# Expert weights split once and kept on chip, and unrolled expert tiles of 128 rows

## The reference

```python
x = x + attn(layernorm(x), W_write, W_read, decay, log_alpha)   # recurrent over chunks
x = x + ffn(layernorm(x), gate_w, w1, b1, w2, b2)

# ffn: 4096 rows, D = 256, F = 1024, E = 8, TOP_K = 2
probs = softmax(x @ gate_w.T); topk_probs, topk_idx = top_k(probs, 2)
h = gelu(w1[topk_idx] @ x + b1[topk_idx])      # per chosen expert
y = w2[topk_idx] @ h + b2[topk_idx]
out = sum over the 2 of y * topk_probs
```

## Time and profile before

| | |
|---|---|
| median of 3 runs | 681.88 us (680.44 to 682.3) |
| span of the profiled execution | 644.7 us, mean granted TensorE clock 0.961 |
| own time of the profiled execution | not listed; the median is 37.2 us over its span |
| PE / PEld busy | 585.2 us (91%) / 502.0 us (78%) |
| DVE busy | 560.0 us (87%) |
| ACT busy | 414.1 us (64%) |
| POOL busy | 291.4 us (45%) |
| recurrent part and tables | up to 222.4 us |
| expert part, PE's matmuls | 222.4 to 632.8 us |

### The profile page before, as it was taken

One profiled execution on the slowest core, in us unless ns is written; L12 is line 12 of the kernel. 1 busy time (PEld: TensorE's weight loads), 2 busy tenths in 40 slices (PEclk: granted clock), 3 DMA queues, 4 the chain that ended last, 5 costly groups with the idle time before them and its releaser, 6 DMA issues.

```text
span 644.7 us, 17218 instructions
## 1 busy us (share of the span) xinstructions
PE 585.2 (91%) x5368; PEld 502.0 (78%) x5368; DVE 560.0 (87%) x1323; ACT 414.1 (64%) x819; POOL 291.4 (45%) x301
## 2 busy tenths in 40 slices
PE   3899889888894499999999999999999999999992
PEld 2677677676673288888888888888888888888882
DVE  4699898998886799999999998999999999999971
ACT  6454554543541487878777777777787877777751
POOL 4145777677667414443343434243433334342433
PEclk9899997999896599999999999999999999999997
DMA  6567464466122415253434434252524343443422
GB/s 231 185 201 280 134 229 165 161 224 205 60 94 96 97 29 84 48 76 51 73 57 67 71 53 77 47 82 47 77 49 74 51 73 57 67 72 52 80 29 33
DMA packets 87098, 63.46 MB, mean 98 GB/s; under 512 B 56224, under 2 KB 79392, under 8 KB 87072
## 3 DMA queue, kind: packets, MB, share of 16 engines
q1 hardware_dynamic: 72768, 44.23, 25.4%
q0 software_dynamic: 14304, 18.92, 17.0%
HBM read 27.36 MB, written 25.53 MB: 82 GB/s over the span
## 4 chain that ended last, share of the span: by engine, by line
PE 61%; POOL 12%; issue 11%; DVE 8%; DMA 5%; ACT 2%; POOLq 0%; DVEq 0%; ACTq 0%; SPq 0%
PE psum L1213 28%; PE psum L1194 28%; POOL sent_rows L469 6%; DMA out<-arena 3%; POOL tiny L448 2%; DMA sent_rows<-arena,tiny 2%; DVE arena L903 2%; POOL arena L477 2%; POOL out L494 1%; PE psum L1139 1%; POOL tiny L445 1%; PE psum L1113 1%; PE psum L1142 1%; DVE arena L819 1%; PE psum L1103 1%
## 5 line engine op out<-in xcount | busy, mean ns | idle before, releaser
L1194 PE MATMUL psum<-arena 128*128 128x256 f16 x1872 | 229.7, 273 | 0.7 <-ACT arena L631 0.7
L1213 PE MATMUL psum<-arena 128*128 128x256 f16 x1872 | 229.5, 273 | 0.4 <-DVE arena L996 0.4
L1009 DVE SCALAR_TENSOR_TENSOR arena<-weights,arena 128x1024 f16<-128x1024 f16 x156 | 190.2, 1221 | 25.0 <-issue 14.1
L494 POOL DMA_INDIRECT out<-arena x78 | 133.3, 1709 | 155.9 <-ACT arena L670 135.4
L1194 PEld LDWEIGHTS psum<-arena 128*128 128x128 f16 x1872 | 183.0, 98 | 23.1 <-DVE arena L1009 0.9
L1213 PEld LDWEIGHTS psum<-arena 128*128 128x128 f16 x1872 | 183.1, 98 | 21.9 <-DVE arena L996 0.7
L651 ACT ACTIVATE arena<-weights 128x1024 f16 x156 | 164.2, 1055 | 35.8 <-PE psum L1213 20.8
L631 ACT ACTIVATE arena<-psum,arena 128x256 f32<-128x256 f32 x312 | 130.7, 470 | 68.3 <-PE psum L1194 63.6
L996 DVE TENSOR_TENSOR arena<-arena 128x512 f16<-128x512 f32 x156 | 108.1, 693 | 5.3
L469 POOL DMA_INDIRECT sent_rows<-arena,tiny x64 | 63.7, 995 | 41.4 <-DVE tiny L778 21.6
L503 POOL COPY arena<-arena 128x2 int32<-128x2 int32 x39 | 24.4, 625 | 107.6 <-DMA out<-arena 98.8
(11 more groups left out here) (129 smaller groups left out, 566.6 us busy)
## 6 DMA issues: line engine op xcount, KB each, us to landing
weights<-in_experts SPq DMA_DIRECT2D x16, 1024.0 KB
arena<-in_b SPq DMA_DIRECT2D x39, 128.0 KB, 2.9
out<-arena SPq DMA_DIRECT2D x17, 256.0 KB, 2.4
arena<-in_x SPq DMA_DIRECT2D x16, 256.0 KB, 2.8
sent_rows<-pad SPq DMA_DIRECT2D x8, 265.0 KB, 7.5
out<-arena POOLq DMA_INDIRECT x78, 4.1
sent_rows<-arena,tiny POOLq DMA_INDIRECT x64
arena<-sent_rows SPq DMA_TRANSPOSE x39, 3.9
```

What stands on the lines that cost most here:

```text
L494: pool.indirect_dma_start(out=out, out_offset=bass.IndirectOffsetOnAxis(ap=tok_cur[:, 1 - par, c:c + 1], axis=0), in_=yout[:, 1 - par, c], ...
L1009: v.scalar_tensor_tensor(out=wcur[:, 1 - par, w + PIECE:w + 2 * PIECE], in0=weights[:, bass.ds(e * EW + part * PIECE, PIECE)], scalar=WSCA ...
L1194: last = pe.matmul(ps_h[:, s, mm], w1_of(par, k, lo, m), tileT[:, par, part], start=(n == 0), stop=(n == 3 * KD - 1))
L1213: last = pe.matmul(ps_y[:, par, c], lhs, w2_of(par, m, lo), start=(m == 0 and n == 0), stop=(m == MF - 1 and n == 2))
```

## The change

All expert weights are split in the recurrent part, two pieces a step, by ACT and DVE. The halves take the place of the f32 weights: piece j arrives one piece further on in `weights` and its halves are written behind it. So `wcur` and the splits per tile are gone. Tiles have 128 rows (NT = (8192 + 8 x 127) // 128 = 71), all loops of the expert part are written out, and PE reads the weights' halves in place, with slices that begin at a register, the expert's number. The hidden rows are handled in 2 groups of 4 blocks. `b2` of all experts is loaded once. DVE multiplies bias and result by the gate, so L670 is gone, and POOL takes the row numbers from `tile_in`, which has 8 buffers, so L503 is gone. There is one indirect addition a tile, and each waits for the one before. Tables are computed in memory that the recurrent part has freed.

The core of the diff; of removed lines only some are shown, and lines with @@ tell the place:

```diff
-TILE = 256
+TILE = 128
...
-EW = 4 * PIECE
+EW = 4 * 2 * PIECE
...
-        weights = sb("weights", [P, E * EW])
+        weights = sb("weights", [P, (NPIECE + 1) * PIECE])
+        halves = weights[:].bitcast(F16)
...
@@ SyncE, recurrent step @@
+                    reached(sp, "wlo_done", 2 * n - 3)
                     src = experts[2 * n:2 * n + 2] if is_int(n) else experts[bass.ds(2 * n, 2)]
-                    o = 2 * n * PIECE
+                    o = (2 * n + 1) * PIECE
...
@@ SyncE, expert part @@
+            sp.wait_ge(buffers_free, 1)
+            sp.dma_start(b2_all, b2.rearrange("e d -> (e d)").rearrange("(a w) -> a w", a=1).to_broadcast([P, E * D])
+                         ).then_inc(b2_in, 16)
             sp.wait_ge(pad_out, 16 * E)
+            def load_tile(i):
+                came(sp, "h_ps", i - 4, 2)
+                r = sp.value_load(tile_row_i[0:1, i:i + 1], min_val=0, max_val=E * CAP - TILE)
+                sp.dma_start_transpose(tileT[:, i % 4], sent16[bass.ds(r, TILE), 0:2 * D]).then_inc(tileT_ld[i % 4], 16)
+                if i >= 8:
+                    sp.wait_ge(added, 16 * (i - 7))
+                sp.dma_start(tile_in[:, i % 8], sent[bass.ds(r, TILE), D:ROW]).then_inc(tile_ld[i % 8], 16)
...
@@ GpSimd, expert part @@
+            def add(i):
+                came(pool, "yout_done", i)
+                pool.wait_ge(tile_ld[i % 8], (i // 8 + 1) * 16)
+                if i > 0:
+                    pool.wait_ge(added, i * 16)
+                pool.indirect_dma_start(
+                    out=out, out_offset=bass.IndirectOffsetOnAxis(ap=tile_in[:, i % 8, E:E + 1].bitcast(I32), axis=0),
+                    in_=yout[:, i % 4], in_offset=None, compute_op=ALU.add).then_inc(added, 16)
...
@@ ScalarE: called twice in each recurrent step from step 1 to 16, after the xT copies and after vals @@
+            def split_high(j, m, mp):
+                loaded(a, w_in[mp], m, mp)
+                reached(a, "wlo_done", j - 1)
+                if not is_int(j):
+                    a.sem_inc(carrier_act, 1)
+                to, frm = j * (2 * PIECE), (j + 1) * PIECE
+                to = halves[:, to:to + PIECE] if is_int(to) else halves[:, bass.ds(to, PIECE)]
+                frm = weights[:, frm:frm + PIECE] if is_int(frm) else weights[:, bass.ds(frm, PIECE)]
+                a.activation(to, frm, ACT.Copy, scale=WSCALE).then_inc(S["whi_done"], 1)
...
@@ ScalarE, expert part @@
+            def gelu(i, q):
+                came(a, "h_ps", i, 2, q)
+                came(a, "prep_done", i)
+                came(a, "split_done", i - 1, 2, q)
+                for m in range(4):
+                    last = a.activation(act[:, q, m * TILE:(m + 1) * TILE], ps_h[:, q, m], ACT.Gelu_apprx_tanh,
+                                        scale=1.0 / WSCALE, bias=b1_cur[:, i % 2, 4 * q + m:4 * q + m + 1])
...
@@ VectorE: called twice in each recurrent step, after the state's sum and after choose() @@
+            def split_low(j):
+                reached(v, "whi_done", j)
...
+                v.scalar_tensor_tensor(out=lo, in0=frm, scalar=WSCALE, in1=hi, op0=ALU.mult,
+                                       op1=ALU.subtract).then_inc(S["wlo_done"], 1)
...
@@ VectorE, expert part @@
+            def prepare(i):
+                e = v.value_load(tile_exp_i[0:1, i:i + 1], min_val=0, max_val=E - 1)
+                came(v, "act_done", i - 2, 2)
+                v.tensor_copy(b1_cur[:, i % 2], b1T[:].rearrange("p e m -> p (e m)")[:, bass.ds(e * MF, MF)])
+                v.wait_ge(tile_ld[i % 8], (i // 8 + 1) * 16)
+                came(v, "yout_done", i - 2)
...
+                v.tensor_scalar(b2_cur[:, i % 2], b2_all[:, bass.ds(e * D, D)], gate_cur[:, i % 2, 0:1], None,
+                                ALU.mult).then_inc(S2["gated_done"], 1)
+            def finish(i):
+                came(v, "l2_done", i, 2)
+                came(v, "gated_done", i)
+                if i >= 4:
+                    v.wait_ge(added, 16 * (i - 3))
+                v.scalar_tensor_tensor(out=yout[:, i % 4], in0=ps_y[:, i % 2], scalar=gate_cur[:, i % 2, 1:2],
+                                       in1=b2_cur[:, i % 2], op0=ALU.mult, op1=ALU.add).then_inc(S2["yout_done"], 1)
+            prepare(0)
+            for i in range(NT + 1):
                 if has(i):
                     split(i, 0)
+                if has(i - 1):
+                    finish(i - 1)
                 if has(i + 1):
+                    prepare(i + 1)
                 if has(i):
                     split(i, 1)
...
@@ TensorE, expert part @@
+            def w1_of(e, k, lo, m):
+                return halves[:, bass.ds(e * EW + ((2 * k + lo) * PIECE + m * P), P)]
+            def w2_of(e, m, lo):
+                return halves[:, bass.ds(e * EW + ((2 * (2 + m // 4) + lo) * PIECE + m % 4 * D), D)]
+            def first(i, e, q):
+                if q == 0:
+                    pe.wait_ge(tileT_ld[i % 4], (i // 4 + 1) * 16)
+                came(pe, "act_done", i - 1, 2, q)
+                for mm in range(4):
...
                         for lo, part in ((0, k), (0, KD + k), (1, k)):
+                            last = pe.matmul(ps_h[:, q, mm], w1_of(e, k, lo, 4 * q + mm), tileT[:, i % 4, part],
                                              start=(n == 0), stop=(n == 3 * KD - 1))
...
+            def second(i, e, q):
+                s = 2 * (i % 2) + q
+                came(pe, "split_done", i, 2, q)
+                if q == 0:
+                    came(pe, "yout_done", i - 2)
+                for mm in range(4):
+                    for n, (half, lo) in enumerate(((h_hi, 0), (h_hi, 1), (h_lo, 0))):
+                        last = pe.matmul(ps_y[:, i % 2], half[:, s, mm], w2_of(e, 4 * q + mm, lo),
...
+            for i in range(NT + 1):
                 if has(i):
+                    e_of[i] = pe.value_load(tile_exp_i[0:1, i:i + 1], min_val=0, max_val=E - 1)
+                    first(i, e_of[i], 0)
                 if has(i - 1):
+                    second(i - 1, e_of[i - 1], 0)
                 if has(i):
+                    first(i, e_of[i], 1)
                 if has(i - 1):
+                    second(i - 1, e_of[i - 1], 1)
```

More of the change, by code:

```diff
@@ L81, in constants @@
     put("token", (q % 2) * T + (q // 2) * P + p)
[L82 to L83 removed]
+    put("padtoken", TOK + p)
+    put("place", p)
     put("step", np.arange(TOK // TILE)[None, :] * TILE)
@@ L242, in build @@
         x_in = [sem(f"x_in{s}") for s in range(2)]
-        w_in = sem("w_in")
+        w_in = [sem(f"w_in{s}") for s in range(2)]
         row_out = [sem(f"row_out{s}") for s in range(2)]
@@ L321, in both @@
             return v[n * P:(n + 1) * P] if is_int(n) else v[bass.ds(n * P, P)]
[L323 to L333 removed]
         def has(i):
[L336 removed]
+            return 0 <= i < NT
         def came(eng, name, i, per=1, k=None):
[L340 removed]
+            if i >= 0:
                 eng.wait_ge(S2[name], i * per + (per if k is None else k + 1))
@@ L682, in _ @@
+            for i in range(NT):
+                gelu(i, 0)
+                gelu(i, 1)
         @block.vector
@@ L1017, in step2 @@
                     split(i, 0)
+                if has(i - 1):
+                    finish(i - 1)
                 if has(i + 1):
-                    split_low(1)
+                    prepare(i + 1)
                 if has(i):
                     split(i, 1)
-                if has(i - 1):
-                    for c in range(2):
-                        came(v, "l2_done", i - 1, 4)
-                        v.wait_ge(b2_in[1 - par], (i - 1 - (1 - par)) * 8 + 16)
-                        if not is_int(i) or i >= 3:
-                            v.wait_ge(added, (i - 2) * 32)
-                        v.scalar_tensor_tensor(out=yout[:, 1 - par, c], in0=ps_y[:, 1 - par, c], scalar=1.0 / WSCALE,
-                                               in1=b2_cur[:, 1 - par], op0=ALU.mult,
-                                               op1=ALU.add).then_inc(S2["ybias_done"], 1)
@@ L1048, in step2 @@
-                if has(i):
-                    split(i, 3)
-            stage_two(v, step2)
         @block.tensor
@@ L1175, in _ @@
                 pe.matmul(psum[:, 0, :], ident16[:], proj16[:, 0, 0], start=True, stop=True)
[L1176 to L1190 removed]
+            pe.wait_ge(S["wlo_done"], NPIECE)
+            def w1_of(e, k, lo, m):
[7 more added lines that the diff above has]
+                for mm in range(4):
                     n = 0
@@ L1193, in first @@
                         for lo, part in ((0, k), (0, KD + k), (1, k)):
-                            last = pe.matmul(ps_h[:, s, mm], w1_of(par, k, lo, m), tileT[:, par, part],
+                            last = pe.matmul(ps_h[:, q, mm], w1_of(e, k, lo, 4 * q + mm), tileT[:, i % 4, part],
                                              start=(n == 0), stop=(n == 3 * KD - 1))
```

298 lines of the change are left out of this document (72 added, 226 removed).

## The result

The changed kernel takes 825.36 us (median of 4 runs, 824.62 to 826.34); the kernel before took 682.09 us beside it (4 runs, 680.44 to 683.91). The ratio is 1.2086, with a 95% interval of 1.204 to 1.2132: 21% slower, 143 us. The profiled execution has a span of 823.0 us and took 824.93 us itself, so only 1.9 us lie outside the span.

What follows compares the result with a forecast made beforehand. PE's array was taken to bound the expert part, DVE nearly the recurrent part. Span 644.7 plus 79.7 (27 + 3 + 52.7 - 3) plus 37.2 around the span gave 762 us, range 674 to 850.

Steps and rivals of the forecast that it cites:

- Part 1: Expert part, array work with 128-row tiles: 5.24 us a tile, 372 us in all, 37 us less than before.
- Part 2: Expert part, register addresses on PE's queue: 48 operations at 0.11 us, queue-limited tile of 6.5 us, 52.7 us more.
- The other terms: PE's queue per tile: expert number load 0.5, extra wait 0.1, dispatch 0.3, register-addressed loads and matmuls 0.3 us.
- The other engines: Expert part: DVE at most 4.3 us, ACT under 3.8, POOL's additions about 4.5, all under the 6.5 us tile.
- Part 3: Recurrent part, weight splits added to 16 steps: 1.7 us a step (1.1 to 2.4), 27 us in all (18 to 39).
- Part 4: Between the parts and at the end: +3 us (0 to 6) before the expert part, -3 us after the last matmul.
- the +3: Between recurrent and expert parts: `b2` broadcast ahead of the first tile's load and larger tables, +3 us (0 to 6).
- The sum's last term: Time around the profiled span: 37.2 us, the runs' median 681.88 less the span of 644.7, added to the total.
- A: Expert part: the array stays the limit at 5.24 us a tile, register operations under 0.084 us; 672 us; chance 0.17.
- B: PE, expert part: each register-addressed load or matmul costs 0.03 to 0.06 us; about 897 to 1050 us; chance 0.13.
- C: Expert part: weight loads bound the short matmuls at 0.085 us, 6.7 us a tile; about 776 us; chance 0.05.
- D: Expert part: POOL's chain of additions decides; at 7 us a tile about 797 us; chance 0.05.

Runs made afterwards that it cites:

- experiment 2: Changed kernel with all PE weight slices at fixed addresses (expert 0's weights) and no load of the expert number on TensorE: 688.96 us.
- experiment 4: Changed kernel with all 32 weight pieces split after the recurrent part instead of in it, and SyncE's wait for the splits removed: 819.07 us.
- experiment 5: Changed kernel with ten extra 512-column matmuls a recurrent step, result overwritten, ahead of PE's wait for the scores: 801.06 us.
- experiment 8: Changed kernel with DVE's split subtraction replaced by a cheaper copy of the high half (wrong low values): 798.12 us.
- experiment 11: Changed kernel with both the ten filler matmuls a recurrent step and the cheap copy in place of DVE's split subtraction: 766.29 us.
- experiment 6: Kernel before the change with six filler matmuls in each recurrent step: 681.67 us against 681.6, ratio 1.0008.
- experiment 3: Changed kernel with only the second layer's weight addresses fixed (expert 0's weights there), leaving 32 register operations a tile: 690.24 us.
- experiment 7: Changed kernel with second-layer high and low weights in one 512-column matmul, 64 matmuls a tile for 72, still 48 register operations: 821.59 us.
- experiment 10: Changed kernel with the second layer's 512-column matmuls and both matmuls of a block sharing one address, 40 register operations a tile: 753.58 us.

## Why the prediction came out as it did

The forecast was 762 us with 674 to 850, slower with 0.85. The direction, the limit of the expert part and the range were right; the middle was 63 us too low. It is the sum of three errors and one in the other direction: +47.8 for the recurrent part with what follows it (77.8 against 30), +48.9 for the expert part, +1.9 at the end, and -35.3 for time around the span (1.9 against 37.2).

**Part 1** was right: 5.24 us forecast for the array, 5.31 measured in experiment 2.

**Part 2**, the deciding step, was right in mechanism and count (48 a tile, queue-limited) and mis-sized in two terms. The price of a register operation was taken as its own 51 ns plus a gap of 0.06 from the earlier trace rows, 0.11 in all. It is 0.124 in a long row of them, although one lasts 46 ns: 5.95 us a tile for 5.3. The gap was read off one place where three helpers' operations follow each other, rounded to 0.1 us; why it is longer among loads and matmuls no run shows. The other terms, 0.5 + 0.1 + 0.3 + 0.3 = 1.2, measured 0.65 + 0.21 + 0.4 = 1.26. The tile is 7.2 us for 6.5, and 0.7 x 71 = 50 us.

**The other engines** kept up, as forecast: DVE 51%, ACT 32% in the expert part.

**Part 3** is the step that failed. "At most 2.4 (nothing hidden)" was no upper bound: the step grew by 5.1 us, twice the work added to DVE. The forecast counted DVE's busy time against the step and stopped there. It left out TensorE's clock. PE waited 0.40 us a step before and 2.70 after; behind the longer wait stands a stretch at 0.55, and the reads and the update in it took 2.9 us longer. It also left out what happens beside the split: POOL's operations at the same time become longer (0.96 to 2.01, 0.72 to 1.84 us), and DVE's small subtraction, shifted onto an operation of POOL, takes 1.72 us for 0.175. Experiment 4 shows that the splits cause it, and experiments 5, 8 and 11 that it has two parts, each about a third of the loss by itself. What the port alone costs was not measured by a run of its own; it is read from timelines.

**Part 4** can't be told from the recurrent part's drain after the last step in this trace. In experiment 4, where that part is as before, the first expert matmul stands 71.9 us later for 72.6 us of splits, which leaves nothing for the +3. The end was -1.1 instead of -3.

**The sum's last term** was wrong. Each profiled execution here took 1.8 to 2.1 us more than its span. The term carried a difference of chips into the forecast, and by luck it hid a third of the other errors. Where the kernel before spends the 35 us on its upper level stays open, as none of its profiles fell there. The nearest is the profile of experiment 6, with six fillers a step and a span of 677.0 us: its expert part takes 410.1 us as in the rows and begins at 254.7 us instead of 222.4, so all of its extra time lies before it, in steps of some 13.5 us. Whether that is the chip or the fillers no run shows.

**The rivals.** A would have needed under 0.084 us an operation and fell: 0.124 to 0.126. B fell with experiments 3 and 7, C with experiment 2. D did not decide: PE's waits in the expert part are for issue, and in experiment 10, at 6.23 us a tile, it waited 1.0 us in all for DVE. The Trainium skill's issue floor of about 20 cycles ("Runtime: NRT & Kernel Launch", Instruction fetch mechanics) is far below what these operations take: by the 1.2 GHz that the prediction names it is an estimate of 0.017 us, against 0.124 measured. Experiment 10 decides for the trace.

## What to carry to other kernels

Count the addresses that a queue must make, not only the matmuls: with 128-row tiles on this array, 32 a tile were hidden and 48 cost 35% over the array's time, and two slices share an operation only when they are written with the same arithmetic. Before work is put into a loop in which an engine looks 90% full, ask which engine will wait longer for it. If that is TensorE, price its next matmuls at half the clock, and look at what POOL runs beside the new DVE operation, and beside those that it shifts. Take the start of the sum and the median of runs from the same level: an execution's own time minus its span was 2 us here, and a larger remainder meant another execution, not overhead.

## What the hardware showed that was not expected

- A register operation of 46 ns on TensorE's queue took 0.124 us from start to start with loads and matmuls between (0.126 by experiments 7 and 10), and the load of a number 0.65 us.
- A stream of 128-column matmuls, each with its own 128x128 weight load, ran at 56 ns a pair (experiment 2).
- One wait of 2.70 us for scores was followed by a stretch at a granted clock of 0.55, in which f32 matmuls took 1.7 times as long (5.27 against 3.12 us).
- A DVE subtraction on 16 elements a partition took 1.72 us instead of 0.175 where it met a subtraction of POOL on 512, and ended with it. It did so nine times in experiment 8, with a split of 0.43 us, and once in experiment 6, with none.
- POOL's power operation on 2 elements a partition took 1.84 us instead of 0.72 beside a DVE split of 1.23 us; with a copy of 0.43 us in its place it took 0.97 at most from 90 to 170 us.
- The same program, unchanged, took 645 to 651 us on two chips and 676 to 685 us on two others, at mean clocks of 0.954 to 0.972 and 0.899 to 0.930. Six fillers a step raised the clock on one of the latter to 0.943 to 0.965 and left the time as it was.
